# A fused embedding, attention and expert kernel: the expert stage taken pair by pair, all split weights kept, routing weights in the activations, results summed in PSUM

## What is computed

```
h = h + attn(layernorm(h))            # W_qk scales per head, avg of wte is taken off V, W_o projects
x = layernorm(h)
scores = softmax(x @ gate_w + gate_b)
w_full = 2.5 * scores, where chosen (4 groups of 8, then 4 experts of 16 by scores + bias), else 0
act[t, e] = silu(x @ Wu[e] + bu[e]) * (x @ Wg[e] + bg[e]) * w_full[t, e]
y = sum over e of act[t, e] @ Wd[e]  + w_full @ bd
y = y + (silu(x @ sWu + sbu) * (x @ sWg + sbg)) @ sWd + sbd
h = h + y
```

## Time and profile before

| | us |
|---|---|
| median of 3 runs (lowest, highest) | 501.29 (500.12, 502.48) |
| the profiled execution | 502.05 |
| its span, first to last instruction | 500.2 |
| TensorE busy | 467.5 (93%) |
| DVE busy | 324.2 (65%) |
| ACT busy | 174.5 (35%) |
| POOL busy | 70.5 (14%) |
| mean granted TensorE clock | 0.963 of full |

### The profile page before, as it was taken

One profiled execution on the slowest core, in us unless ns is written; L12 is line 12 of the kernel. 1 busy time (PEld: TensorE's weight loads), 2 busy tenths in 40 slices (PEclk: granted clock), 3 DMA queues, 4 the chain that ended last, 5 costly groups with the idle time before them and its releaser, 6 DMA issues.

```text
span 500.2 us, 8643 instructions
## 1 busy us (share of the span) xinstructions
PE 467.5 (93%) x2672; PEld 400.7 (80%) x2672; DVE 324.2 (65%) x860; ACT 174.5 (35%) x566; POOL 70.5 (14%) x94
## 2 busy tenths in 40 slices
PE   5688999999999999999999998599999999999994
PEld 2365768967689766896668988599999999999994
DVE  6875787166861668527657847876666766667664
ACT  1364466045660455605420214122223222222221
POOL 6031111211112111000001422010000100001000
PEclk9798999999999999999979978899999999999997
DMA  8989999999999999650000000011111111111103
GB/s 207 250 267 208 212 209 203 205 212 211 212 213 212 213 213 213 137 95 1 1 0 1 1 21 1 9 36 42 32 29 37 36 40 32 29 37 36 24 1 89
DMA packets 30450, 52.86 MB, mean 106 GB/s; under 512 B 8342, under 2 KB 22479, under 8 KB 30045
## 3 DMA queue, kind: packets, MB, share of 16 engines
q0 software_dynamic: 7664, 39.98, 38.7%
q1 hardware_dynamic: 21548, 11.42, 9.1%
q10 hardware_dynamic: 1216, 1.21, 0.9%
HBM read 50.12 MB, written 1.09 MB: 102 GB/s over the span
## 4 chain that ended last, share of the span: by engine, by line
PE 85%; DVE 8%; issue 2%; ACT 2%; POOL 2%; DVEq 0%; POOLq 0%; ACTq 0%
PE bank L873 13%; PE bank L769 12%; PE bank L727 6%; PE bank L842 4%; PE bank L844 4%; PE bank L846 4%; PE bank L843 4%; PE bank L672 4%; PE bank L845 4%; PE bank L674 4%; PE bank L732 3%; PE bank L684 2%; PE bank L685 2%; PE bank L700 2%; PE bank L728 2%
## 5 line engine op out<-in xcount | busy, mean ns | idle before, releaser
L873 PE MATMUL bank<-wdn,hidT 128*128 128x192 f32 (+1 forms) x408 | 78.8, 330 | 5.9 <-DVE hidT L1101 5.9
L577 ACT ACTIVATE area_b<-bank,bcol 128x356 f32<-128x356 f32 x68 | 38.0, 558 | 132.2 <-PE bank L846 132.2
L1282 DVE SCALAR_TENSOR_TENSOR R<-bank,wts,R 128x192 f32<-128x192 f32 (+1 forms) x204 | 72.5, 411 | 8.1 <-issue 3.7
L495 ACT ACTIVATE pm<-bank,nmax 128x128 f32<-128x128 f32 x96 | 33.9, 365 | 112.0 <-DVE nmax L1010 112.0
L873 PEld LDWEIGHTS bank<-wdn,hidT 128*128 128x128 f32 (+1 forms) x408 | 67.5, 184 | 6.5 <-DVE hidT L1101 6.4
L1101 DVE SCALAR_TENSOR_TENSOR hidT<-bank,bcol,area_b 128x356 f32<-128x356 f32 x68 | 39.9, 587 | 49.0 <-PE bank L846 49.0
L769 PE MATMUL bank<-woT,oT 128*128 128x192 f32 (+1 forms) x432 | 71.6, 327 | 0.0
L769 PEld LDWEIGHTS bank<-woT,oT 128*128 128x128 f32 (+1 forms) x432 | 69.9, 182 | 0.5
L842 PE MATMUL bank<-xah,wah 128*128 128x356 f32 x136 | 54.4, 400 | 0.4 <-DVE lg L1059 0.4
L423 POOL DMA_DIRECT2D wacc<-in_L_attn_wte_dram x26 | 31.4, 1207 | 135.0 <-DMA wacc<-in_L_attn_wte_dram 135.0
L844 PE MATMUL bank<-xah,wal 128*128 128x356 f32 x136 | 45.2, 332 | 0.0
(11 more groups left out here) (183 smaller groups left out, 773.7 us busy)
## 6 DMA issues: line engine op xcount, KB each, us to landing
wacc<-in_L_attn_wte_dram POOLq DMA_DIRECT2D x28, 1344.0 KB, 12.6
woT<-in_L_attn_W_o_dram SPq DMA_DIRECT2D x1, 1728.0 KB, 16.7
oT<-in_x_dram SPq DMA_DIRECT2D x4, 384.0 KB, 9.4
wdn<-in_L_ffn_Wd_dram SPq DMA_DIRECT2D x16, 96.0 KB, 1.9
wacc<-wacc POOLq DMA_DIRECT2D x1, 1344.0 KB, 9.8
wra<-in_L_ffn_Wu_dram SPq DMA_DIRECT2D x16, 64.0 KB, 1.8
wrb<-in_L_ffn_Wu_dram SPq DMA_DIRECT2D x32, 32.0 KB, 2.1
wra<-in_L_ffn_Wg_dram SPq DMA_DIRECT2D x16, 64.0 KB, 1.9
```

The source lines that it names most:

```text
L577: act.activation(sil[:, sl, :], bank[sl][:, 0:CW], ACT.Silu, bias=bcol[:, (n // PAIRS) % 2, 0:1]).then_inc(silu_ready, 1)
L873: last = pe.matmul(o, hidT[:, sl, at:at + rows], wdn[:, k, :], start=True, stop=True)
L1282: last = dve.scalar_tensor_tensor(out=old, in0=src, scalar=wts[0:rows_, 3 * i + t, bass.ds(e, 1)], in1=old, op0=ALU.mult, op1=ALU.add)
```

## The change

- The loops are turned round: pair by pair, and in it expert by expert (17 steps, `STEPS`), written out in full instead of in loops.
- All 17 experts' weights are kept in SBUF. The host packs them into one array `experts` of 706 columns (up, gate, stacked second halves, down, two biases), one DMA each: eight after the `wte` sum has been folded, nine after the last scores, in the places of `qa`, `qb` and others. They are split once, in the steps of pair 0 (three in the last attention pair).
- `gather` is gone. `weigh` multiplies the SiLU result by the routing weights, which SP has spread over all partitions: rows of `wT` go to DRAM (`rows`) and come back as a broadcast of one row, through a ring of four. The down products of all experts of a pair are summed in banks 4 and 5, behind the bias products (`down_biases`); `finish` adds them to `R` once.
- Routing is done per pair (three tiles): for pair 0 in the last attention pair and the hand-over, for the others in the steps k = 8 to 13 of the pair before. Its exponential is made on POOL, as e to the power of the logits, instead of on ACT.
- The table's mean and its correction move from the end of the last attention pair to its units 0 to 2, the sums of W_o to the pair before.
- The output of pairs 0 to 2 is written during the stage, in another layout, which the host puts right.

```diff
+            def exps_of_gates(i):
+                pool.wait_ge(nmx_ready, i + 1)
+                pool.tensor_tensor(sc[:], ebase[:], lg[:], ALU.pow).then_inc(gexp, 1)
...
+            for i in range(PAIRS):
+                sp.wait_ge(wT_ready, i + 1)
+                sp.dma_start(rows[i], wT[0:NE, i % 2, :]).then_inc(wrow_out, 16)
+                sp.wait_ge(wrow_out, 16 * (i + 1))
+                for e in range(NE):
+                    m = NE * i + e
+                    if m >= RING:
+                        sp.wait_ge(weighted, m - RING + 1)
+                    sp.dma_start(wbc[:, m % RING, :], rows[i, e:e + 1, :].broadcast_to([P, CW])).then_inc(wbc_in[m % RING], 16)
...
                     if u == 3 and not last:
                         turn_in(0, 2 * i + 2, i + 1)
+                    if u == 1 and last:
+                        mean()
+                    if u == 2 and last:
+                        mean_projected()
                     if u == 4 and last:
-                        mean()
+                        turn_a(0)
                     turn_probs(u, U + u)
...
-                    project(U, (((turn_ffn, 0),), ((turn_ffn, 1), (gate, 0), (turn_ffn, 2)), ((gate, 1),)))
+                    gate(0)
+                    project(U, True)
...
+            def down_biases(i):
+                pe.wait_ge(wT_ready, i + 1)
+                pe.wait_ge(*((out_read, 3 * i) if i else (proj_read, 3 * PAIRS)))
+                for t, (at, n) in enumerate(COLS):
+                    pe.matmul(out_of(t, n), wT[:, i % 2, at:at + n], bdx[:], start=(t != 1), stop=False, skip_group_check=True)
+
+            def down(n):
+                sl, e = n % 2, n % STEPS
+                pe.wait_ge(hid_ready, n + 1)
+                for t, (at, rows_) in enumerate(COLS):
+                    last = pe.matmul(out_of(t, rows_), hidT[:, sl, at:at + rows_], wdn(e), start=False,
+                                     stop=(e == STEPS - 1), skip_group_check=True)
+                last.then_inc(down_done, 1)
+
+            up_gate(0)
+            for i in range(PAIRS):
+                for k in range(STEPS):
+                    n = STEPS * i + k
+                    if n + 1 < STEPS * PAIRS:
+                        up_gate(n + 1)
+                    if i + 1 < PAIRS:
+                        if k == 3:
+                            turn_a(i + 1)
+                        if k == 5:
+                            turn_b(i + 1)
+                        if k == 7:
+                            gate(i + 1)
+                        if k == 13:
+                            turn_rows(i + 1)
+                    if k == 0:
+                        down_biases(i)
+                    down(n)
...
+            def weigh(n):
+                m = n - n // STEPS - 1
+                dve.wait_ge(silu_ready, n + 1)
+                dve.wait_ge(wbc_in[m % RING], 16 * (m // RING + 1))
+                dve.tensor_tensor(sil[:, n % 2, :], sil[:, n % 2, :], wbc[:, m % RING, :], ALU.mult).then_inc(weighted, 1)
...
+            def finish(i):
+                dve.wait_ge(down_done, STEPS * (i + 1))
+                for t in range(3):
+                    n = COLS[t][1]
+                    src = bank[4][:, t * E:(t + 1) * E] if t < 2 else bank[5][0:n, 0:E]
+                    dve.tensor_tensor(R[0:n, 3 * i + t, :], src, R[0:n, 3 * i + t, :], ALU.add).then_inc(out_read, 1)
...
+            for i in range(PAIRS):
+                for k in range(STEPS):
+                    n = STEPS * i + k
+                    if k:
+                        weigh(n)
+                    fuse(n)
+                    if i == 0 and k + WAH0 < NW:
+                        w_stack(k + WAH0)
+                    if k == 0 and i:
+                        finish(i - 1)
+                    if i + 1 < PAIRS:
+                        if k == 0:
+                            correct(i + 1)
+                        if k == 2:
+                            experts_in(i + 1)
+                        if k == 8:
+                            logits(i + 1)
+                            softmax_start(i + 1)
+                        if k == 9:
+                            softmax_end(i + 1)
+                        if k == 10:
+                            choose_groups()
+                        if k == 11:
+                            choose_experts(i + 1)
+            finish(PAIRS - 1)
```

More of the change, by code:

```diff
@@ L39, in early_fusion_kernel @@
 def early_fusion_kernel(nc, x, txt, tok_W, tok_b, tok_pos, tok_cls, ln_w, W_qk, W_o, wte,
-                        gate_w, gate_b, bias, Wu, bu, Wg, bg, Wd, bd, sWu, sbu, sWg, sbg, sWd, sbd, out):
+                        gate_w, gate_b, bias, experts, bdown, rows, out):
     PAIRS, _, KX, _ = x.shape
@@ L50, in early_fusion_kernel @@
     V = wte.shape[0]
-    NE = Wu.shape[0]
-    HID = Wu.shape[2]
+    NW, _, WX = experts.shape
+    NE = NW - 1
+    HID = P
     GRP = 4
@@ L771, in project @@
                         last.then_inc(wo_done, 1)
-                    for step, k in between[t] if between else ():
-                        step(k)
+                    if t == 1 and last_pair:
+                        turn_rows(0)
             turn_in(0, 0, 0)
@@ L848, in expert_in, with products @@
[L848 to L858 removed]
+            def products(dst, c, i, e):
+                o, p = dst[:, 0:CW], i % 2
+                high, low, both = wah(e)[:, c], wal(e)[:, c], wbs(e)[:, c]
+                pe.matmul(o, high, xah[:, p], start=True, stop=False)
+                pe.matmul(o, high, xal[:, p], start=False, stop=False)
+                pe.matmul(o, low, xah[:, p], start=False, stop=False)
+                pe.matmul(o, both, xbh[:, p], start=False, stop=False)
+                return pe.matmul(o, both, xbl[:, p], start=False, stop=True)
@@ L862, in up_gate @@
                 if n >= 2:
-                    pe.wait_ge(hid_ready, st_ - 1)
-                products(bank[2 + sl], 1, n % PAIRS, k).then_inc(gt_ready, 1)
-            def down(n, st_, k):
-                sl = n % 2
-                pe.wait_ge(hid_ready, st_ + 1)
-                for t, (at, rows) in enumerate(COLS):
-                    if n >= 2 and t != 1:
-                        pe.wait_ge(acc_done, 2 * (st_ - 1) - (1 if t == 0 else 0))
-                    o = bank[4 + sl][:, t * E:(t + 1) * E] if t < 2 else bank[6 + sl][0:TT, 0:E]
-                    last = pe.matmul(o, hidT[:, sl, at:at + rows], wdn[:, k, :], start=True, stop=True)
-                    if t >= 1:
-                        last.then_inc(down_done, 1)
@@ L1192, in _ @@
-            start = own.at
-            per = UPP + (4 + 4) + 4
-            with dve.Fori(0, PAIRS - 2) as i:
-                own.restart(per * i + start)
-                pair(i, False, True)
-                assert own.n == per
-            own.restart(start + per * (PAIRS - 2))
-            pair(PAIRS - 2, False, False)
-            pair(PAIRS - 1, True, False)
-            logits(1)
-            correct(3)
-            experts_in(3)
-            logits(2)
-            features_out(3)
-            dve.wait_ge(wd_in[0], 16 * DLOADS)
```

707 lines of the change are left out of this document (312 added, 395 removed).

## The result

The changed kernel takes **512.5 us** (median of 4 runs, 512.09 to 512.58) beside 501.8 of the kernel before on the same chip: ratio 1.0216, interval 1.0189 to 1.0244. It is 2.2% slower where 488 was forecast, 24.5 us above it; the time is close to that of rival A (514). The profiled execution took 512.49 us, span 510.7.

A forecast was written before the change was run, and what follows sets the result against it. TensorE paces the expert stage (68 steps by 2.60 = 176.9 us stay), gains lie at its ends: -7.3 - 0.4 + 0 + 1.6 - 6.9 = -13.0, so 488; range 481 to 497 (0.52), 8 in 10 481 to 518.

The forecast's parts named there:

- rival A: POOL's power grows with its elements to 8.5 us and holds DVE; kernel slower, 514 us; chance 0.33, from 500 to 522.
- the power on POOL: Softmax exponential, 48 elements on POOL: low end 0.9 us, high end 8.5, taken as 2; 0 us in the sum.
- Weighing in, gather out: Expert steps: three 0.41 us updates go, one 0.52 us multiply comes, off the path; slack 1.4 us.
- Hand-over 20.0: From last attention matmul to first expert product: 20.0 us instead of 27.3, so -7.3 us.
- What moves into the stage: Transposes and gates of pairs 1 to 3 add 8.1 us, bias products 3.9; expert stage 188.9 us.
- Routing in DVE's steps: Routing operations in steps k = 9 to 11 and k = 0 stall 4.8 us; stage 193.7, so -0.4 us.
- rival B: Stalls at the steps larger: forty small DVE operations cost 0.1 more each, with clock drops, 11 us: 499; chance 0.12.
- Weights and rows by DMA: Expert weight loads and spread routing rows stay hidden; rows asked for 7.8 us ahead, may take 4.
- Attention: Transposes for pair 0 and the mean, correction and normalisation moved into the attention part cost +1.6 us.
- Tail: After the last down projection: 3.4 us instead of 10.3, so -6.9 us.
- Rival C: The moved work costs nothing, no stalls in expert steps or attention: 482 us, low end of the forecast's range (0.52).
- D: Rival: unrolled steps, run once each, are late from instruction memory; inside the forecast range, no separate chance.

The follow-up runs named there:

- e1: The change with the exponential of all pairs on ACT instead of POOL's power: 495.3 us, 0.9867 of the kernel before.
- e5: The change with all exponentials on ACT and the expert and group choices cut in halves over k = 10 to 13, transposes at k = 15: 488.5 us.
- e4: The change with POOL's power over 24 instead of 48 elements, so routing uses wrong scores: 495.3 us (one run).
- e3: The change with the exponentials of pairs 1 to 3 on ACT, pair 0's still on POOL: 502.1 us (one run).
- e6: The change with the power kept on POOL, its result asked for three steps later (k = 12), choices at 13 and 14: 499.4 us (one run).
- e8: The change with the power kept on POOL, the choices cut in halves over k = 10 to 13, transposes and rows at k = 15: 512.9 us (one run).
- e7: e1 with a ring of two spread routing rows instead of four: 494.6 us (one run).

## Why the prediction was wrong

The direction was wrong by one term of the sum, the power on POOL, put at nothing; a second was too small, a third (the attention) too large by 1.2; the others hold.

1. *Weighing in, gather out*: right. The multiply takes 0.547 us (0.52 from the earlier trace rows), quiet steps keep 2.60.
2. *Hand-over 20.0*: right as a path. From the gate of pair 0 to the first expert product e1 and e5 take 19.7 us (267.53 to 287.20 in e1) and the change 25.7; of the 6.0 between them 4.2 is the stall for `wts` and 1.45 the slower block behind it.
3. *What moves into the stage*, 8.1 + 3.9: right within half a microsecond in each pair (47.9 reckoned, 48.4 measured in e5).
4. *Routing in DVE's steps*: **too small**. The bursts themselves were sized well: the group choice takes 2.8 and the expert choice 2.9 us (281.13 to 283.96 to 286.82), reckoned 2.7 and 2.6. But e1's stage is 201.3, 7.6 above the 193.7. The idle time is 6.1 instead of 4.8: 2.16 in the first pair where 2.2 was reckoned, and 0.44 at k = 0 instead of 0.8, but 1.75 in each of the next two pairs where 0.9 was reckoned. The other 6.3 is time in which TensorE counts as busy. 3.9 of it e5 has too, whose clock is at 1.00 in the whole stage (1.5 of them belong to point 3, 1.3 more lie in the first pair and 1.0 before the first and behind the last bias product); some 1.7 is the 3.4 us of work at half clock behind the stall of 2.16; 0.7 stays open. Spreading took back 6.5 (e5). The time is two thirds of the way to rival B (499, e1 495.3), but B's premise, operations dearer by 0.1 each, came true at most in the first pair, where e1's group choice takes 3.5 us beside 2.8 in the next; its clock drop came true once instead of three times.

```profile
326.47 2.29 PE L901 MATMUL bank<-area_a,area_b 128*128 128x192 f32 x6 [2.16 <-DVE area_b L1105]
```

   The row is e1's: after a wait of 2.16 us the six passes take 2.29 instead of 1.14.
5. *The power on POOL*: **the step that failed.** "I take 2 us, near the low end, since the only wide POOL row streams". It takes 8.06, and e4 shows it to be a price for each element. The two rows of the same operation gave 8.5; the prediction had reckoned itself that their difference speaks for the high end, and it let a row of another operation, a subtraction, overrule them. The kernel before has eight such rows:

```profile
L416 POOL TENSOR_TENSOR rs<-ve,mhalf 128x4 f32<-128x4 f32 x4 | 5.2, 1289 | 6.3 <-DVE ve L978 6.3
L416 POOL TENSOR_TENSOR rs<-ve,mhalf 128x3 f32<-128x3 f32 x4 | 3.4, 855 | 75.1 <-DVE ve L978 75.1
```

   Those of 3 elements take 0.85 to 0.87 us, those of 4 take 1.04 to 1.52, so any pair of them gives 0.17 or more for one element and the high end or more for 48; none speaks for 2 us. That the high end came out within 0.5 us is luck: the means give 0.43 for one element, some 20 us for 48, and the change's own means (1.16 and 1.03) give 0.12. Over wider steps the price is steady, 0.15 from 4 to 24 elements and 0.16 from 24 to 48. The rule that was weighed there says that a dependent fp32 chain costs four cycles for each element (the Trainium skill, GPSIMD Engine Reference, Performance pitfalls for Q7 kernels). A price that grows with the elements does not contradict it, but how many links a power has the rule doesn't give, and whether such a chain is the cause no run here shows.
   Its consequence was reckoned well: 5.6 in the hand-over (measured 6.0), and for the stage 24.6 with step 4 (measured 212.8 - 188.9 = 23.9). But the split was not: with the power gone 11.5 of it goes (19.8 reckoned), and 12.4 stay (4.8), among them 6.1 of idle time and the 6.3 of busy time of point 4. Power and small operations share the slack: spreading alone gives 0.7, spreading after the power is gone 6.5; both together give 18.0. Which is charged first is a matter of order.
6. *Weights and rows by DMA*: right, hidden. The rows land in 3.1 us (reckoned 4), the 353 KB of an expert in 5.0 to 7.5.
7. *Attention* +1.6: measured +0.4 between two single executions; its clock alone moves it by more than that in kernels with the same attention (2.6 us between e1 and e3), so whether the moved work cost anything stays open.
8. *Tail* 3.4: measured 3.3.

Rival C (everything free, 482) did not occur; D left no trace: in the change no expert step of the first pass waits for anything but DVE.

## What to carry to other kernels

Look for the price of a moved operation on its new engine in rows of this very operation, not in those of another one, and read all of them. Rows of 3 and 4 elements don't give a reliable price for 48, but when all of them speak against a cheap operation, a size in the middle is worth timing first: e4's 24 elements would have settled it. A slow operation on an idle engine is free only as long as nobody in a full queue asks for its result before it is there: put the wait behind as much other work as the operation lasts (e6), and look at what then comes later (there the routing rows), or give the operation to the engine that has it cheap, table loads included (e1). And when the main stall is large, a cure of the small ones shows nothing (e8); try it again once the large one is gone (e5).

## What the runs showed of the hardware

- A power on POOL takes 1.03 (3 elements of a partition), 1.16 (4), 4.21 (24) and 8.06 us (48): 0.15 to 0.16 us for each further element from 4 on. ACT makes 48 exponentials in 0.24 us, plus two table loads of 1.28.
- TensorE's granted clock falls to 0.50 (1.2 GHz) around every stall of the change of 3.4 to 4.2 us, before TensorE restarts or up to 1 us after, and 3.4 to 5.4 us of work run at it. The same follows e1's stall of 2.16 us (3.4 us of work) and e7's of 1.97 (0.50 from 328 to 331). Behind stalls of 1.1 us and less (e5, and e6's of 1.04) it stays at 1.00 in the whole stage.
- The clock granted early in the program differs between kernels whose code is the same up to there (0.57 to 0.70 from 20 to 30 us) and shifts all that follows by up to 2.6 us, as much as some of the effects looked for. Differences under 3 us between single runs are to be read from a mark inside the program.
